# Edge-attribute products of a two-layer GNN: low weights on half the rows, second bias by TensorE

## What is computed

```python
h = maximum(layernorm(x), 0)
edge_feat = concatenate([h[src], h[dst], edge_attr], axis=-1)   # 512 + 512 + 64
m = mish(edge_feat @ W1 + b1)                                    # 20000 x 512
messages = mish(m @ W2 + b2)                                     # 20000 x 512
agg = segment_sum(messages, dst)
u = mish(concatenate([h, agg], axis=-1) @ W3 + b3)
x = x + layernorm_affine(h + u @ W4 + b4)
```

## Time and profile before

| | |
|---|---|
| median of 3 runs (lowest, highest) | 1102.37 us (1102.1, 1102.68) |
| profiled execution | 1102.44 us, span of its instructions 1100.6 us |
| TensorE products / weight loads | 1044.5 us (95%) / 874.1 us (79%) |
| VectorE / ScalarE / GpSimd | 878.8 us (80%) / 886.0 us (80%) / 727.3 us (66%) |
| mean granted clock of TensorE | 0.985 |

### The profile page before, as it was taken

How to read it: one execution, slowest core, us unless ns; L and a number is a source line. 1 busy time by engine, 2 the same in 40 slices (tenths; PEclk the granted TensorE clock), 3 DMA queues, 4 the chain that set the end, 5 groups by cost and what they waited for, 6 DMA issues and landing times. The chain is left out here.

```text
span 1100.6 us, 18555 instructions
## 1 busy us (share of the span) xinstructions
PE 1044.5 (95%) x5641; PEld 874.1 (79%) x5642; DVE 878.8 (80%) x1504; ACT 886.0 (80%) x1081; POOL 727.3 (66%) x638
## 2 busy tenths in 40 slices
PE   3578999999999999999999999999999999999997
PEld 1126889998889888888888888888888888888796
DVE  7998536635526399999999999999999999999786
ACT  6985735624503799999999999999999999999584
POOL 6875438631255587777888888888877777760217
PEclk9959999999999999999999999999999999999999
DMA  2005962751265387766666666676666666661002
GB/s 105 8 1 141 179 217 83 255 181 48 77 227 117 90 175 154 156 144 141 141 141 138 133 141 145 131 142 138 141 139 139 143 145 136 142 127 39 1 1 94
DMA packets 79458, 137.43 MB, mean 125 GB/s; under 512 B 10731, under 2 KB 36588, under 8 KB 79286
## 3 DMA queue, kind: packets, MB, share of 16 engines
q0 software_dynamic: 38048, 87.58, 39.4%
q1 hardware_dynamic: 41366, 49.32, 13.9%
HBM read 113.33 MB, written 18.29 MB: 120 GB/s over the span
## 5 line engine op out<-in xcount | busy, mean ns | idle before, releaser
L766 POOL DMA_INDIRECT gather_pq<-q_table,dst x157 | 310.9, 1980 | 57.3 <-issue 47.5
L758 POOL DMA_INDIRECT gather_pq<-p_table,src x157 | 179.2, 1141 | 104.0 <-PE banks L1118 50.3
L1136 PE MATMUL banks<-w_lo,h_hi 128*128 128x512 f32 x620 | 243.2, 392 | 1.3 <-DVE banks L2139 1.2
L1137 PE MATMUL banks<-w_hi,h_hi 128*128 128x512 f32 x620 | 241.9, 390 | 0.0
L1141 PE MATMUL banks<-w_hi,h_lo 128*128 128x512 f32 x620 | 166.1, 390 | 0.0
L1136 PEld LDWEIGHTS banks<-w_lo,h_hi 128*128 128x128 f32 x620 | 116.4, 188 | 29.5 <-issue 7.4
L1141 PEld LDWEIGHTS banks<-w_hi,h_lo 128*128 128x128 f32 x620 | 116.4, 188 | 24.4
L1137 PEld LDWEIGHTS banks<-w_hi,h_hi 128*128 128x128 f32 x620 | 116.4, 188 | 23.2
L2110 DVE SCALAR_TENSOR_TENSOR h_full<-mish_work,banks 128x512 f32<-128x512 f32 (+1 forms) x154 | 98.4, 681 | 38.2 <-ACT mish_work L1446 35.1
L2135 DVE SCALAR_TENSOR_TENSOR message<-mish_work,banks 128x1024 f32<-128x1024 f32 x78 | 95.3, 1222 | 8.4 <-ACT mish_work L1470 0.3
L1111 PE MATMUL banks<-ident,gather_pq 128*128 128x128 f32 x628 | 96.5, 276 | 0.8 <-DMA gather_pq<-q_table,dst 0.4
(11 more groups left out here) (272 smaller groups left out, 2668.0 us busy)
## 6 DMA issues: line engine op xcount, KB each, us to landing
edge_attr<-in_edge_attr_t SPq DMA_DIRECT2D x20, 256.0 KB, 2.9
attr_high<-edge_attr_hi SPq DMA_DIRECT2D x40, 128.0 KB, 2.0
attr_low<-edge_attr_lo SPq DMA_DIRECT2D x40, 128.0 KB, 1.8
edge_attr_parts<-attr_high SPq DMA_DIRECT2D x79, 64.0 KB, 2.4
edge_attr_parts<-attr_low SPq DMA_DIRECT2D x79, 64.0 KB, 2.2
x_nodes<-h_hi POOLq DMA_DIRECT2D x10, 256.0 KB, 14.9
x_nodes<-h_lo POOLq DMA_DIRECT2D x10, 256.0 KB, 7.8
p_table<-p_stage SPq DMA_DIRECT2D x10, 256.0 KB, 2.0
```

The source lines that it names most:

```text
L758: nc.gpsimd.indirect_dma_start(GP[:, 2 * j + k, :], None, p_tab[:, :], bass.IndirectOffsetOnAxis(ap=SRC[:, 2 * s + k:2 * s + k + 1], axis= ...
L766: nc.gpsimd.indirect_dma_start(GP[:, 2 * j + k, :], None, q_tab[:, :], bass.IndirectOffsetOnAxis(ap=DST[:, 2 * s + k:2 * s + k + 1], axis= ...
L1136: pe.matmul(at, h_high(s, j)[:, c, e], W2_LO[:, c, :], start=False, stop=False, skip_group_check=True)
L1137: pe.matmul(at, h_high(s, j)[:, c, e], W2_HI[:, c, :], start=False, stop=False, skip_group_check=True)
```

## The change

Three things change together.
- The low-weight products use only the high part of the attributes, on 64 rows each. Blocks 0 and 1 (bank 0) take rows 0 to 63 of WE_LO and AT_R; blocks 2 and 3 (bank 1) take rows 64 to 127 of WE_LO and of a new buffer AT_R2, which holds the high part on those rows. They stand last in z1 in two pairs: (block 0, block 2), (block 1, block 3). What low weights x low attributes gave is left out.
- SP loads AT_R2 with a third transfer of 64 KB per step, so a slot's semaphore counts 48 and not 32. AT_R2 lies on AT_HI and AT_LO, which are free by then.
- TensorE makes the second tile's bias by a product in every step; `b2_second_tile`, its semaphore and waits go.

```diff
+        AT_R2, _ = sb("edge_attr_high_again", [P, SLOTS, PW], F32R, at=place[0] - 4 * 2 * PW)
         AT_LO, _ = sb("edge_attr_lo", [P, 2, PW], F32R)
...
                 for rows, table in ((slice(0, EDGE_DIM), at_tabs[0]), (slice(EDGE_DIM, P), at_tabs[1])):
                     sp.dma_start(AT_R[rows, j, :].bitcast(F32),
                                  table[bass.ds(s, 1), :, :].rearrange("o p e -> (o p) e")).then_inc(attr_in[j], 16)
+                sp.dma_start(AT_R2[EDGE_DIM:P, j, :].bitcast(F32),
+                             at_tabs[0][bass.ds(s, 1), :, :].rearrange("o p e -> (o p) e")).then_inc(attr_in[j], 16)
...
                     for c in (2 * b, 2 * b + 1):
-                        for w in (WE_HI, WE_LO):
-                            mm = pe.matmul(Z1v[:, c, 0:P * tiles(s)], w[:, c * P:(c + 1) * P], AT_R[:, slot, 0:P * tiles(s)],
-                                           skip_group_check=True, start=False, stop=(w is WE_LO and c == 2 * b + 1))
+                        pe.matmul(Z1v[:, c, 0:P * tiles(s)], WE_HI[:, c * P:(c + 1) * P], AT_R[:, slot, 0:P * tiles(s)],
+                                  skip_group_check=True, start=False, stop=False)
+                for k in range(2):
+                    for b, rows, high in ((0, slice(0, EDGE_DIM), AT_R), (1, slice(EDGE_DIM, P), AT_R2)):
+                        c = 2 * b + k
+                        mm = pe.matmul(Z1v[:, c, 0:P * tiles(s)], WE_LO[rows, c * P:(c + 1) * P], high[rows, slot, 0:P * tiles(s)],
+                                       skip_group_check=True, start=False, stop=(k == 1))
                 mm.then_inc(z1_done, 1)
...
                 if after(s, 2) and k == 0:
                     pe.wait_ge(b2_first, s - 1)
-                elif after(s, 2) and j == 0:
-                    pe.wait_ge(b2_second, s)
                 else:
                     pe.matmul(at, ONES_R[:, :], B2_R[:, :], start=True, stop=False, skip_group_check=True)
...
-                edge_step(s, s, 64, 32, None)
+                edge_step(s, s, 64, 48, None)
...
-            def b2_second_tile(s, j):
-                nc.scalar.copy(Z2[:, 2 * j + 1, :], B2_ROW[:, 0, :]).then_inc(b2_second, 2)
-
...
                     sq2(s - 2)
-                if j == 1 and after(s, 3) and live(s - 1) and tiles(s - 1) == 2:
-                    b2_second_tile(s - 1, 1 - j)
-                if live(s - 2):
                     log2(s - 2)
...
-            act.wait_ge(b2_in, 16)
```

More of the change, by code:

```diff
@@ L413, in gnn_kernel @@
         h_full = [sem(f"h_full_{h}") for h in range(2)]
-        z2_done, b2_in, b2_first, b2_second = (sem(n) for n in ("z2_done", "b2_row_in", "b2_in_first_tile", "b2_in_second_tile"))
+        z2_done, b2_in, b2_first = (sem(n) for n in ("z2_done", "b2_row_in", "b2_in_first_tile"))
         b_exp, b_sq, b_ln, b_r, msg_full, msg_hi, msg_lo = (sem(n) for n in
@@ L1196, in _ @@
                         s = Z1_BEHIND.index(n)
-                        z1(s, s, 64, 32)
+                        z1(s, s, 64, 48)
             z2(0, 0, 0)
             for s in range(2, SLOTS):
-                edge_step(s, s, 64, 32, None)
+                edge_step(s, s, 64, 48, None)
             with pe.Fori(1, EDGE_PAIRS // SLOTS) as i:
                 for j in range(SLOTS):
-                    edge_step(SLOTS * i + j, j, 64 * (i + 1), 32 * (i + 1), 2 * i + (j - 4) // 2)
+                    edge_step(SLOTS * i + j, j, 64 * (i + 1), 48 * (i + 1), 2 * i + (j - 4) // 2)
             for s in range(EDGE_PAIRS - EDGE_PAIRS % SLOTS, EDGE_PAIRS + 4):
-                edge_step(s, s % SLOTS, 64 * (s // SLOTS) + 32 * tiles(s), 32 * (s // SLOTS + 1), (s - 4) // 2)
+                edge_step(s, s % SLOTS, 64 * (s // SLOTS) + 32 * tiles(s), 48 * (s // SLOTS + 1), (s - 4) // 2)
             idle_products(1, IDLE_AG)
```

## The result

| | before | after |
|---|---|---|
| median of 6 runs each (lowest, highest) | 1102.53 us (1100.69, 1109.72) | 1121.55 us (1119.27, 1122.69) |
| span of the profiled execution | 1100.6 us | 1118.9 us |

The ratio is 1.0161, with a 95% interval of 1.0144 to 1.0178: some 18 us slower, where 6.9 us faster was forecast. The range given did not hold it.

The account below looks back on a forecast made before the run. Two equal loops bound it: TensorE alone (16.73 us per pair of steps) and z1-ScalarE-VectorE. Ordinary pairs -3.4, stretched (GpSimd splitting w3) -3.2, ramp and rest -0.3: -6.9 from 1102.4 gives 1095.5 us; range 1093.3 to 1113.5.

Parts of the forecast that it names:

- x: The time by which z1, a step's attribute stage on TensorE, becomes shorter; forecast 0.20 us.
- rival 3: In z1, the halves run one after the other, x = 0: +5.2 us, 1107.6 us; chance 0.06.
- PE's room: TensorE's slack in pairs of steps where GpSimd splits w3: about 0.34 us with a cast, 0.15 taken for the rest.
- The low products: In z1, four products of 0.12 us become two pairs; x = 0.24 if halves and weight loads run at once.
- Rival 1: In z1, weight loads take turns, x = 0.04: 1105.3 us; chance 0.15.
- The two changes of tile: Switches between 128 and 64 rows in each step's z1: 0.02 us each, 0.04 a step.
- Rival 2: Tiling changes around z1's low products drain the array, 0.16 us each: +11.0 us, 1113.4 us; chance 0.23.
- The bias product: Between z1 and the segment sums, TensorE gains 0.23 us in every even step, only in its own loop.
- Its copy: Second tile's bias copy leaves ScalarE, 0.52 us of starts a pair of steps; gives nothing by itself, ScalarE being full.
- exp2: ScalarE's even-step operation waiting for z2, which the bias puts 0.03 us later; hidden by 0.43 us of room.
- the order in z1: Bank 1's transposes start 0.68 us after z1's start instead of 0.97, needing full1's second half; hidden by 0.14 us.
- the third load: SP's extra attribute transfer, 0.6 us of each 8.4 us step, 2.6 us before the loop; costs nothing.

Follow-up runs that it names:

- e9: Kernel before with TensorE making the second bias in all steps and the low products of blocks 0 and 2 left out, all on 128 rows: 1094.32 us.
- e2: Kernel before with TensorE making the second bias in all steps, without ScalarE's copy; attribute products as before: 1107.58 us, ratio 1.0047.
- e4: Changed kernel with all four low products on the lower 64 rows, so no two can run at once: 1140.53 us, ratio 1.0333.
- e6: Kernel before with unread 128-row and 64-row products of several widths and mixes behind its last one: alternating-half pairs take 0.23, 0.12, 0.11 us at 512, 256, 128 columns.
- e8: Kernel before without ScalarE's copy of the second bias and with no product in its place: 1103.11 us, ratio 1.0000.
- e10: Kernel before with the low products of blocks 0 and 2 left out and ScalarE's bias copy kept: 1095.56 us, ratio 0.9938.
- e3: Changed kernel with its low products on all 128 rows again, in the new place, third load kept: 1109.76 us, ratio 1.0051.
- e7: Kernel before with rounds behind its last product, four full products then 1, 2, 4 or 8 64-row pairs: 1.45, 1.56, 1.79, 2.29 us a round.

## Why the prediction was wrong, point by point

- **What bounds the kernel: held.** PE's own loop and the loop through z1, ScalarE and VectorE, both at 16.7 us, gave the right sum wherever x was known: e9 (x = 0.24: -8.6 us measured, -9.1 by the prediction's sum) and e2 (x = 0, 5.2 us measured; the prediction's rival 3, which is the same sum, had 5.2). After the change PE's loop alone counts, 17.35 us: 16.75 + 0.22 + 2 x 0.155 = 17.28, and 0.07 in small widenings, up to 12 ns each, of the products behind. One reading of the rows was wrong without harm: not every other stretched pair has a cast, each has one (16 starts of L789 from 528.7 to 784.4 us, 17.05 apart). The pairs do alternate in length, 17.17 and 16.88 us, so PE's room is 0.42 and 0.13 us where the prediction took 0.34 and 0.15.
- **The low products: the best case was right.** "If the halves run at once and their weights load at once, 2 x 0.12, so x = 0.24": e4 and e6 show both. Rival 1, loads that take turns, is out. The 0.11 us of the earlier trace rows is the rate of loads for the same rows; it does not bind across halves.
- **The two changes of tile: the step that failed.** The prediction took 0.02 us each, "the nearest row is the alternation with transposes", and 0.16 as the upper bound, "the tail of a product". Measured: 0.195 to 0.20 each. The alternation of transposes and products keeps the 128 rows, so it was no neighbour at all; even its 0.04 us was the wait for h_full, as z1 of 892.29 has 0.66 us for its first transposes where the others have 0.60. And the bound from above was too low, as it counted one loss and the intervals show two: the first product on the other side comes 0.09 us late (0.211 against 0.118), and the second one too (0.224 against 0.118; at the exit 0.208 and 0.337 against 0.118 and 0.235). The load rows above fit this: the first weights behind a change are not loaded ahead but start with their product, and the second product then waits for a load that could start only 0.11 us after the first (899.14 behind 899.03; in e6 0.105 us). That is read from the spacing of starts; no run separates it from other causes.
- With x = 0.24 - 0.39, taken unrounded as -0.155, the prediction's own rule gives 20 x (0.23 + 0.31) + 8 x (0.54 - 0.34) + 8 x (0.54 - 0.15) = +15.5 us. The rest, up to the span's 18.3, lies outside the 35 pairs (18.3 - 16.6 = 1.7 us, of which the sum has one pair) and in the small widenings of the products behind, 0.07 us in an ordinary pair. **Rival 2** named the place, from high to low products and from these to what follows, and a cost for the change, and gave 1113.4 us with 0.16 a change; its sign, a gap over 0.06 us at both ends, came. The Trainium skill's rule (TensorEngine Tiling (Array Packing), Tiling Modes), that changing the mode drains TensorE, agrees with the 0.195 to 0.20 us of a change; that it is a drain, and all of it, these traces do not show. The other one cited (TensorE: Matmul & The Clock Gate, Part 3), products on different row groups some 4 ns apart with overlapping loads, agrees with the trace: 3 ns. The forecast's x of 0.20 stands near what the second alone would give; the first, which had no number, got a chance of 0.23, and the sum took a change at 0.02.
- **The range.** It ended at the full drain of 0.16 with loads at once, 1113.5 us, and left out what lay beyond as a case of its own, at 1128. The chances had given rival 2 changes of up to 0.2 us, which the range did not take in. A price without any row should have had its upper end behind both losses, the tail and a load that is not made ahead.
- **The bias product**: 0.22 to 0.23 us an ordinary pair, nothing in a stretched one: right. **Its copy**: gives nothing by itself (e8), right; "ScalarE is full today, so without this a shorter PE loop would stop at it" was wrong by at least 0.17 us a pair (e10: 16.56 instead of 16.73).
- **exp2, the order in z1, the third load**: each hidden, as said. e3 shows no cost of place, order and load together beyond its interval. SP's q_table stores now begin at 316.97 instead of 314.11, but the last ends at 334.83 instead of 334.56, and the first z1 starts at 344.37 instead of 344.28.

## What to carry to other kernels

Pairs on half the rows are worth one product per pair, and each visit to them costs a fixed 0.4 us here, so by these numbers a visit has to hold more than three pairs of 256 columns (0.4 / 0.12) before it pays. In e7, 8 pairs with four full products take 2.29 us, where 16 full products of 256 columns in their place would take 4 x 0.23 + 16 x 0.12 = 2.8; no kernel with such a run was tried. Gather such products into long runs, or leave them on the full array. Before an edit that puts a new mode of an engine into a stream, price the way in and out by itself, with a row of products behind the kernel; that takes one run. A row is a neighbour of an unknown cost only if it changes the same thing.

## What the runs showed of the hardware

- Two changes of tile cost 0.4 us together, independent of how many pairs lie between (e7, 1 to 8), and of whether both halves or one are used (1.56 us a round, as with pairs).
- The weights of the two halves load at once (starts 3 to 4 ns apart in the changed kernel and, at 256 columns, in e6); on one set of rows new weights came every 0.11 us at the fastest (128 columns, e6 and the earlier trace rows).
- In e6 the clock fell: granted 0.93 of 2.4 GHz over 1108 to 1118 us and 0.50, that is 1.2 GHz, from 1118 to 1135, with PE shown busy without a gap, while e7's longer rounds kept 2.4. Before it fell the engine had changed its tile every 0.31 us from 1111.0 to 1116.6 us, in rounds of one full product and one pair, then of one full and one 64-row product, all of 256 columns; behind it such an interval takes 0.51 us. It is a single run, and nothing was varied to find the cause. The windows (window, length, PE, PEld, DVE, ACT, POOL busy, clock, DMA share, GB/s):

```profile
1108.00:1118.00 10.00, 10.00 (x66) 7.09 (x65) 0.00 (x0) 0.00 (x0) 0.00 (x0) 0.93 0.01 2
1118.00:1135.00 17.00, 17.00 (x36) 7.72 (x35) 0.00 (x0) 0.00 (x0) 0.00 (x0) 0.50 0.00 0
```
